# Differential attention with a gated feed-forward: packed diagonal blocks, value projections moved, work redistributed over the units

## The reference, cut to what matters

```python
xn = layernorm(x)                                   # x: 1 x 1024 x 256, float32
q1, k1, q2, k2, v = split(xn @ Wqkv)                # 16 heads; q, k: 8 wide; v: 16 wide
A1 = softmax(causal(q1 k1^T / sqrt(8))) @ v
A2 = softmax(causal(q2 k2^T / sqrt(8))) @ v
diff = A1 - lam * A2                                # lam from four vectors of 8
diff = 0.8 * normalise(diff) ; attn = diff @ Wproj  # rms norm over the 16 values of a head (0.8 stands for 1 - LAMBDA_INIT)
ffn = (gelu(fp8(xn) @ fp8(Wg0)) * (fp8(xn) @ fp8(Wg1))) @ fp8(Wlin)
out = x + attn + ffn
```

## Time and profile before

| | |
|---|---|
| median of 3 runs | 198.92 us (198.6 to 199.15) |
| profiled execution, its own time | 199.27 us |
| its span, first to last instruction | 197.5 us |
| PE busy | 182.2 us, 92% |
| ACT busy | 163.6 us, 83% |
| DVE busy | 92.4 us, 47% |
| POOL busy | 59.4 us, 30% |
| first exponential of a unit starts | 38.01 us |
| last exponential of a unit ends | 180.5 us |
| last value product ends | about 182.75 us |

### The profile page before, as it was taken

One profiled execution on the slowest core, in us unless ns is written; L12 is line 12 of the kernel. 1 busy time (PEld: TensorE's weight loads), 2 busy tenths in 40 slices (PEclk: granted clock), 3 DMA queues, 4 the chain that ended last, 5 costly groups with the idle time before them and its releaser, 6 DMA issues.

```text
span 197.5 us, 3554 instructions
## 1 busy us (share of the span) xinstructions
PE 182.2 (92%) x1446; PEld 78.3 (40%) x1450; DVE 92.4 (47%) x218; ACT 163.6 (83%) x136; POOL 59.4 (30%) x71
## 2 busy tenths in 40 slices
PE   6899989899999999999989999999998999899940
PEld 6855334454332323242333424344342423233830
DVE  0975798431223240540472025216703697895840
ACT  2156865899999999999999999999999899998010
POOL 8526600042216142314442043235216124320000
PEclk9999999999999999999999999999999999999997
DMA  5967377780000000000277781000000000000051
GB/s 174 404 242 245 73 179 205 207 190 10 0 0 3 0 0 3 0 0 3 60 203 188 181 191 39 0 3 0 0 3 0 0 3 0 0 3 0 0 178 44
DMA packets 8149, 14.99 MB, mean 76 GB/s; under 512 B 1984, under 2 KB 5312, under 8 KB 8128
## 3 DMA queue, kind: packets, MB, share of 16 engines
q1 hardware_dynamic: 7440, 14.05, 25.5%
q10 hardware_dynamic: 688, 0.66, 1.0%
HBM read 5.26 MB, written 1.05 MB: 32 GB/s over the span
## 4 chain that ended last, share of the span: by engine, by line
PE 74%; ACT 15%; DVE 4%; POOL 1%; issue 1%; POOLq 0%; DVEq 0%
PE ps L910 29%; PE ps L898 17%; ACT probs L442 13%; PE ps L752 8%; PE ps L758 4%; PE ps L941 4%; PE ps L747 3%; PE ps L851 3%; PE ps L813 3%; DVE area L529 2%; DVE o_t L594 1%; ACT probs L430 1%; PE ps L742 1%; PE ps L947 1%; ACT L430 1%
## 5 line engine op out<-in xcount | busy, mean ns | idle before, releaser
L442 ACT ACTIVATE probs<-ps,shift 128x1536 f32<-128x1536 f32 x96 | 140.1, 1554 | 2.4 <-PE ps L898 1.6
L910 PE MATMUL ps<-probs,v_all 128*32 128x512 f32 (+3 forms) x768 | 78.1, 496 | 1.5 <-DVE o_t L594 1.5
L366 POOL TENSOR_SCALAR_AFFINE_SELECT probs<-probs 128x1024 f32<-128x1024 f32 (+1 forms) x40 | 36.7, 917 | 109.7 <-ACT probs L442 109.6
L898 PE MATMUL ps<-q_st,k_st 32*128 32x512 f32 (+3 forms) x384 | 49.8, 420 | 1.2 <-issue 0.8
L898 PEld LDWEIGHTS ps<-q_st,k_st 32*128 32x128 f32 x384 | 22.4, 182 | 58.6 <-ACT probs L442 30.4
L594 DVE STREAM_TRANSPOSE o_t<-ps 128x512 f32<-128x512 f32 x16 | 11.5, 717 | 49.5 <-PE ps L910 49.5
L910 PEld LDWEIGHTS ps<-probs,v_all 128*32 128x32 f32 x768 | 16.4, 108 | 19.6 <-issue 13.9
L752 PE MATMUL ps<-xn_t,w_q 128*128 128x512 f32 (+1 forms) x38 | 17.3, 557 | 0.8 <-ACT xn_t L393 0.8
L813 PE MATMUL ps<-area 128*128 128x512 fp8e4 x64 | 14.5, 379 | 1.0 <-DVE area L529 1.0
L430 ACT ACTIVATE probs<-ps 128x512 bf16<-128x512 f32 x16 | 9.3, 597 | 4.5 <-PE ps L813 2.7
L529 DVE TENSOR_TENSOR area<-ps,probs 128x512 fp8e4<-128x512 f32 x16 | 10.5, 687 | 1.8 <-ACT probs L430 1.7
(11 more groups left out here) (78 smaller groups left out, 117.2 us busy)
## 6 DMA issues: line engine op xcount, KB each, us to landing
q_st<-parts SPq DMA_DIRECT2D x32, 128.0 KB, 2.8
k_st<-parts SPq DMA_DIRECT2D x32, 128.0 KB, 2.8
probs<-L_ffn_w_gating SPq DMA_DIRECT2D x4, 512.0 KB, 7.8
probs<-L_ffn_w_linear SPq DMA_DIRECT2D x1, 1024.0 KB, 13.1
w_q<-L_attn_Wqkv SPq DMA_DIRECT2D x2, 384.0 KB, 5.8
out<-probs SPq DMA_DIRECT2D x3, 256.0 KB, 3.0
x_sb<-L_attn_x SPq DMA_DIRECT2D x2, 256.0 KB, 4.2
x_sb<-L_attn_x ACTq DMA_DIRECT2D x2, 256.0 KB, 4.5
```

The lines of the kernel that those rows point to most:

```text
L366: pool.affine_select(out=blocks, in_=blocks, pattern=pattern, compare_op=ALU.is_ge, fill=0.0, base=0, channel_multiplier=-1).then_inc(mask ...
L442: act.activation(probs[:, at:at + PER_UNIT, :].rearrange("p s u -> p (s u)"), ps[:, 3 * (n % 2):3 * (n % 2) + 3, :].rearrange("p b n -> p ...
L898: ins = pe.matmul(ps[:, bank, at:at + wide * P], k_st[rows, g % STACKS, kb * P:(kb + 1) * P], q_st[rows, g % STACKS, queries], start=True, ...
L910: ins = pe.matmul(ps[32 * j:32 * j + 32, 6, q0 % HALF:q0 % HALF + wide * P], v_all[:, g % HG, kb, 32 * j:32 * j + 32], probs[:, slot + j, ...
```

## The change

The rows of x are laid on partitions in another order. Of each 256 rows, quarters of 64: even blocks hold quarters 0 and 1, odd blocks quarters 3 and 2. The two halves of a diagonal block that still need masking can then share columns: for two diagonal blocks (256 columns) only 192 are kept, with the first 64 queries of the one in the upper 64 partitions and those of the other in the lower 64. Two groups of heads are laid out together, in 17 chunks of 512 columns where there were 18. Four pairs of groups give 68 chunks, 272 items, and 92 units: 90 of three items, one of one and one of two at the middle.

- A chunk with diagonals has nine pieces: eight of 64 columns and one of 128. So `score` issues nine matmuls per head, two of them with 64 keys as weights and the others with 128. The value product reads the shared strips twice, with two sets of values (`FULL`, and `EARLY`, which has zeros in one half of the partitions).
- There are four such chunks in each pair of groups, and POOL masks each with two instructions on 64 partitions, each over 4 heads, 4 strips and 64 columns.
- Value weights are 17 columns wide, not 32.
- The value projections of blocks 2 to 7 are ahead of the feed-forward part on PE, and ACT copies them out of PSUM, where DVE did. DVE makes the `EARLY` set with four copies.
- The projections of branch 2's queries and keys begin in unit 0, each in one matmul group of 512 columns; norms and down projections have other units, and a down projection is no longer split over two units.
- The loads of x and the stores of the result are twice as many, each of 64 partitions.

```diff
-VW = 32
+VW = DV + 1
+def diagonal(at, a, c):
+    b, d = a + 1, c + 1
+    return [(at, b, FULL, b * P, MINOR), (at + 64, d, FULL, d * P, MINOR),
+            (at + 128, b, EARLY, b * P + MINOR, MINOR), (at + 128, a, EARLY, a * P, MINOR),
+            (at + 192, d, EARLY, d * P + MINOR, MINOR), (at + 192, c, EARLY, c * P, MINOR),
+            (at + 256, a, FULL, a * P + MINOR, MINOR), (at + 320, c, FULL, c * P + MINOR, MINOR)]
 CHUNKS = [
+    [(0, 0, diagonal(0, 0, 2) + [(384, 2, FULL, 384, 128)])],
+    [(0, 0, [(0, 0, FULL, 128, 384), (384, 1, FULL, 256, 128)])],
+    [(0, 0, [(0, 1, FULL, 384, 128)]), (0, 1, [(128, 4, FULL, 640, 384)])],
+    [(0, 1, [(0, 0, FULL, 512, 512)])],
...
+MASKED = (0, 7, 9, 11)
+OPENS = ((0, 0), (2, 1), (8, 1), (10, 1))
+CLOSES = ((2, 0), (8, 0), (10, 0), (16, 0))
+STARTS = list(range(0, ITEMS // 2, 3)) + [ITEMS // 2] + list(range(ITEMS // 2 + 2, ITEMS, 3)) + [ITEMS]
+QK_AT = {0: (4, 0), 1: (4, 1), 5: (5, 0), 8: (5, 1), 13: (6, 0), 17: (6, 1), 25: (7, 0), 29: (7, 1)}
+NORM_AT = {4: 0, 12: 1, 21: 2, 33: 3}
+DOWN_AT = {37: 0, 41: 1, 45: 2, 49: 3, 54: 4, 58: 5, 62: 6, 66: 7}
+LATER = {20: 6, 26: 6, **{k: 4 for k in range(57, 63)}, 63: 3, 64: 3, 65: 3, 66: 2, 67: 2}
+def due(k):
+    return last_unit(k) + LATER.get(k, 5)
...
# SP (the loads by ACT and the stores are doubled in the same way)
+            for i in (0, 2):
+                for p0, rows in halves:
+                    sp.dma_start(x_sb[p0:p0 + MINOR, 2 * i:2 * i + 2, :], x_rows[:, i, rows, :]).then_inc(x_in[i], 16)
# POOL
+                for p0, first in ((0, 0), (MINOR, P)):
+                    strips = probs[p0:p0 + MINOR, at:at + J, first:first + 4 * MINOR].rearrange(
+                        "p j (s u) -> p j s u", s=4)
+                    pool.affine_select(out=strips, in_=strips, pattern=[[0, J], [0, 4], [1, MINOR]],
...
# ACT
+            upper(3)
+            square_of(3)
+            for b in (2, 4, 6):
+                values_in(b)
# DVE
+                for p0 in (0, MINOR):
+                    first = b + p0 // MINOR
+                    dve.tensor_copy(v_all[p0:p0 + MINOR, EARLY, :, first:first + 3:2, :],
+                                    v_all[p0:p0 + MINOR, FULL, :, first:first + 3:2, :]).then_inc(early_out, 1)
# PE, ahead of the feed-forward part
+            for b in range(2, TB):
+                if b >= 4 and b % 2 == 0:
+                    pe.wait_ge(v_out, b - 2)
+                project_values(b)
# PE, scores
+                for p in range(max(len(h) for h in heads)):
+                    for h in heads:
+                        if p < len(h):
+                            ins = score(*h[p], general)
+            def score(g, j, bank, piece, general):
+                at, kb, part, q0, wide = piece
+                rows, queries = slice(32 * j, 32 * j + 32), slice(q0, q0 + wide)
+                keys = MINOR if part == EARLY and kb % 2 == 0 else P
+                out = ps[0:keys, bank, at:at + wide]
+                ins = pe.matmul(out, k_st[rows, g % STACKS, kb * P:kb * P + keys], q_st[rows, g % STACKS, queries],
+                                start=True, stop=not general)
# PE, values
+                for at, kb, of, q0, wide in pieces:
+                    for j in range(J):
+                        ins = pe.matmul(ps[32 * j:32 * j + VW, 6, q0 % HALF:q0 % HALF + wide],
+                                        v_all[:, of, g % HG, kb, VW * j:VW * j + VW], probs[:, slot + j, at:at + wide],
+                                        start=first, stop=False, skip_group_check=True)
+                    first = False
# PE, beside a unit
-                for b in V_AT.get(n, ()):
+                    ins = queries_keys(u, 7, k, 0, HALF)
```

More of the change, by code:

```diff
@@ L686, in _ @@
             bound(dve, own, 1)
+            keep(2, 1)
+            down(0)
             keep(3, 0)
@@ L904, in scores @@
-                ins.then_inc(scores_ready, 1)
-            def product(g, c, at, kb, wide, q0, start):
-                slot = (g * NC + c) % KEPT * J
-                for j in range(J):
-                    ins = pe.matmul(ps[32 * j:32 * j + 32, 6, q0 % HALF:q0 % HALF + wide * P],
-                                    v_all[:, g % HG, kb, 32 * j:32 * j + 32], probs[:, slot + j, at:at + wide * P],
-                                    start=start, stop=False, skip_group_check=True)
-                return ins
@@ L931, in second_half @@
-            def second_half(g):
-                first, (kb, wide, q0) = CHUNKS[MIXED]
-                pe.wait_ge(o_taken, 2 * g + 1)
-                product(g, MIXED, first[1] * P, kb, wide, q0, True)
+                heads = []
+                for e, item in enumerate(range(STARTS[n], STARTS[n + 1])):
+                    k, j = item // J, item % J
+                    heads.append([(2 * (k // NC) + gi, j, 3 * (n % 2) + e, piece)
+                                  for gi, _, pieces in CHUNKS[k % NC] for piece in pieces])
@@ new lines, in values @@
+            def values(k, part):
+                c, slot = k % NC, k % KEPT * J
+                gi, h, pieces = CHUNKS[c][part]
+                g = 2 * (k // NC) + gi
+                if c in MASKED:
+                    pe.wait_ge(masked, masks_until(k))
+                else:
+                    pe.wait_ge(exp_done, last_unit(k) + 1)
+                if k == 0:
+                    pe.wait_ge(v_ones, 1)
+                    pe.wait_ge(zeros_set, 1)
+                    pe.wait_ge(v_out, TB)
+                    pe.wait_ge(early_out, 2)
+                if k == 7:
+                    pe.wait_ge(early_out, 4)
+                first = (c, part) in OPENS
+                if first and (g, h) != (0, 0):
+                    pe.wait_ge(o_taken, 2 * g + h)
+                for at, kb, of, q0, wide in pieces:
[4 more added lines that the diff above has]
+                    first = False
+                if (c, part) in CLOSES:
+                    ins.then_inc(o_ready, 1)
@@ L950, in values_due @@
             def values_due(n, first, end):
-                for g in range(first, end):
-                    for c in range(NC):
-                        if due(g, c) == n:
-                            values(g, c)
-                        if c == MIXED and due(g, c) + 1 == n:
-                            second_half(g)
+                for k in range(first, end):
+                    for part in range(len(CHUNKS[k % NC])):
+                        if due(k) + part == n:
+                            values(k, part)
             def attention(br, general):
```

325 lines of the change are left out of this document (147 added, 178 removed).

## The result

The changed kernel takes **224.59 us** (median of 4 runs, 224.16 to 225.72), beside 199.03 us (198.6 to 199.22) for the kernel before on the same chip: ratio 1.130, 95% interval 1.126 to 1.133. The forecast was 217, its range 203 to 226. The direction and the main cause were right; the size was 7.6 us short. The profiled execution's span went from 197.54 to 223.2 us, +25.7.

What follows compares the result with a forecast made beforehand. The prediction took PE as the bound from unit 6 on, ACT 4% behind; terms 5.3 ahead, 0 in units 0 to 5, 12.4 from unit 6 and 1.0 ending sum to +18.7, 217.6, said as 217 us, range 203 to 226.

Steps and rivals of the forecast that it cites:

- The rival at 192: Whole kernel: ACT sets the pace, so packing its exponentials shortens the units, 192 us; chance 0.09 with mixtures near it.
- Scores: 0.93 us for a unit with a diagonal: PE's scores: weight loads pace nine short pieces, so a diagonal unit takes 0.93 us against 0.43.
- the term +12.6: PE's scores from unit 6 on: longer diagonal units add 12.6 us, of +13.5 over all units.
- the rival at 206 to 207 us: PE's scores: short pieces cost only their columns, so the kernel takes 206 to 207 us; chance 0.15.
- Values: 1.25 for a diagonal chunk: PE's value products: 640 columns and 18 steps make 1.25 us a diagonal chunk, +0.7 us in all.
- The feared floor of 0.107 for a set of four heads: Value products: no set under 0.107 us, +14; with 64-column weights draining PE as alternative, 230 to 236 us, chance 0.11.
- the lower bound I had kept: Value products: 17-column weights could save the first load's 0.03 us, 80 times, -1 us.
- Transposition waits: +3.5: PE at the bank's transposition, from unit 6 on: 7 more waits of 0.5 us, +3.5 us.
- Ahead of the units: +5.3: Before the units: 24 value-projection matmuls +5.2, earlier gelu -0.4, more loads of x +0.5, together +5.3 us.
- Units 0 to 5: 0: First units: ACT sets the pace, so the value projections leaving PE buy nothing, 0 us.
- the clock 0.03: PE's clock falls to 1.2 GHz in stretches of short pieces, over 225 us; chance 0.03.
- Ending: +1.0: End of the kernel: twice as many stores on SP, partly hidden by the additions, +1.0 us.

Runs made afterwards that it cites:

- values_back: Changed kernel with the value projections of blocks 2 to 7 back beside units 0 to 5, copied out by DVE: median 224.66 us.
- long_first: Changed kernel with the 128-column piece of a diagonal chunk first among a head's nine score pieces, not last: 226.57 us.
- before_vw17: Kernel before with value weights of 17 columns, not 32, and nothing else changed: 198.25 us against 199.25.
- opens_later: Changed kernel with products of chunks lying over two accumulation halves further apart, closing part one unit earlier, opening part one later: 224.56 us.
- before_short_pieces: Kernel before with scores of two of a group's nine chunks in eight matmuls of 64 columns per head, not one of 512: 217.37 us.

## Why the prediction was right, and where its size came short

Parts measured by themselves: short score pieces 17.1 us (in the changed kernel), value projections ahead 6.5 and transfers 2.3 (in the kernel before). Together 25.9, of 25.6 measured. That they meet so well is partly luck, because the parts do not simply add: taken out of the changed kernel, the move of the value projections gives nothing by the median (values_back), or 1.7 us once the short pieces are gone. With both undone 6 us remain, of which the transfers are 2.3. The other 4 belong to the rest (values read twice, masks in two instructions, projections in other units), and they were not taken apart.

**PE is the bound, ACT is not.** Shown for the changed kernel. ACT's idle time before the exponentials grew to 22.9 us, and with the score pieces and the start undone the packing bought 0.7 us from unit 6 on. The rival at 192 fell. But with them undone PE is no bound either: both have some 122 us of work in 131.7. The rival went by ACT's sum alone, and what the engines wait for each other was not in it.

**Scores: 0.93 us for a unit with a diagonal.** The mechanism is shown twice, by narrower weights (1.04 to 0.72) and by short pieces in the kernel before (0.43 to 1.01). The value was 1.04, so the term +12.6 was too small by about 30 x 0.11 = 3.3 us, which is what the whole stretch from unit 6 on was short by. (By its own figures the prediction's term is 56.8 - 42.9 = 13.9, and 12.9 from unit 6 on, not 13.5 and 12.6; that hides 0.3 of it.) Three things in the records make the 0.11. A set of three 128-column loads follows the last at 0.112, not 0.107, so the ninth load starts at 0.78, not 0.75. Its matmul starts 0.03 after it, not 0.06. And the last matmul's start is followed by the next work's only 0.24 us later, where I had counted 0.107 for its columns. The mis-sized step is this tail, and it is not the time of the last piece's columns: after a last piece of 64 columns (long_first) it is still 0.21. What it is made of no run here shows.
The Trainium skill (TensorE: Matmul & The Clock Gate, LDWEIGHTS) gives the time of a weight load as its columns over 1.2, in ns, whatever the number of rows: 107 for 128 and 53 for 64 columns. The trace agrees, 0.112 and about 0.058 between sets. The rule cited in the prediction (the Trainium skill, TensorEngine Tiling (Array Packing), Instruction Overhead) is that a matmul of one column takes as long as one of 60; it says nothing of the load. Here the load decides, and the rival at 206 to 207 us fell. The Trainium skill (TensorEngine Tiling (Array Packing), Key Properties) says that a change of tiling mode drains the engine. Between 128- and 64-column loads no drain shows: the ninth load starts at 0.78 us, which is six steps of 0.112 and two of 0.058.

**Values: 1.25 for a diagonal chunk.** Measured 1.24. The feared floor of 0.107 for a set of four heads isn't there: a 64-column set takes half of it. Normal products gained 0.013 by the 17-column weights, worth 1.0 us by themselves (before_vw17), the lower bound I had kept.

**Transposition waits: +3.5.** They came, 3.9 us in 7 places by the view of waits, where it was 1.5 in 3. What the time owes to them is not shown: opens_later left 4.2 us of them in place and was 1.5 us faster up to unit 70.

The stretch's other terms (whole projections -3.7 and -0.4, a norm -0.3) were not measured one by one.

**Ahead of the units: +5.3, measured +6.0.** The 24 matmuls took 5.18, as said. The loads of x were the term mis-sized: four issues on SP take 2.99 us, where two took 0.95, and the first projection starts 1.06 us later, not 0.5.

**Units 0 to 5: 0, measured +2.1.** This is the step that failed in kind. "ACT sets the pace, so they buy nothing" was right of the matmuls, and wrong of what their leaving does. In the changed kernel PE is idle for most of 48 to 50 us, and the clock falls:

```profile
46.00:48.00 2.00, 1.61 (x14) 0.60 (x12) 1.82 (x5) 2.00 (x2) 0.85 (x1) 1.00 0.07 14
48.00:50.00 2.00, 0.50 (x3) 0.19 (x3) 0.10 (x1) 2.00 (x3) 1.85 (x3) 0.82 0.00 0
50.00:54.10 4.10, 2.81 (x7) 0.90 (x8) 0.69 (x1) 3.03 (x3) 0.64 (x1) 0.50 0.00 0
54.10:57.00 2.90, 2.90 (x79) 2.07 (x78) 0.00 (x0) 1.54 (x1) 0.00 (x0) 0.66 0.00 0
```

At 1.2 GHz a projection took 2.08 us instead of 1.06, scores 0.73 instead of 0.43, the first diagonal values 1.81 instead of 1.24. I had given the clock 0.03, and looked for its fall in stretches of short pieces. It fell where PE had too little to do. The same was shown in the kernel before, by moving the six projections away and nothing else. All seven profiles with the value projections ahead have this fall, and none of the six that have them beside the units. Beside it stands a wait of 2.1 us for the squares, which POOL now makes behind a mask twice as long; I had called POOL hidden and had not looked at what else its queue carries in the first units. Taking it away brought unit 6 forward by 1.0 us (2.0 by the medians of the whole), and the clock fell all the same.

**Ending: +1.0, measured +2.1.** The work on PE is the same as before; the stores take longer. But 2.1 is one execution's figure. From the end of the last value product to the end of the span it takes 14.7 to 14.9 us in the four profiles with five stores and 14.8 to 17.0 in the nine with ten, on average 1.0 more. So the term was right on average, and the profile after shows a long one.

## What to carry to other kernels

Where a matmul has fewer columns than the weights in front of it, count loads and their width, not columns: with weights of 128 columns, eight pieces of 64 took 1.01 us where one of 512 took 0.43. Before work is moved off a matmul engine that seems to have it for nothing, ask whether the engine stays busy without it: in the kernel before the move cost 5.2 us where the work went and another 1.3 where it had been. Where two engines are within a few per cent of each other, work taken from the one behind gives next to nothing (7.6 us of ACT's, 0.7 of the stretch), and a sum for each engine alone is too low: with 122 us of work for both the stretch took 131.7.

## What the runs showed of the hardware

- The clock of PE fell to its lower level behind light stretches: from 49 to 56 us in the changed kernel (and from 48 to 55 when the squares came earlier), and from 45 to 55 us in the kernel before without its value projections beside the units. Twice it fell at 180 us (long_first, opens_later), behind ten microseconds in which exponentials set the pace and PE was busy 8.6 and 8.5 of 10.2 us. The changed kernel's profiled execution has the same ten microseconds, with the same 8.6, and its clock stayed up; why it fell in the one and not in the other is open. In the 32 units of short pieces in before_short_pieces, with PE busy 78.78 of 80 us, it never fell.
- The packed kernels vary more: 221.25 to 225.92 us for one of them, roughly in the order of its mean clock, where the kernel before stays within 1.2 us. Falls of the clock in some executions and not in others can make that, and so can the doubled transfers: with them alone the kernel before varies by 2.5 us, and the endings in the profiles by 2.2. The two were not told apart.
- Weight loads of successive pieces of one head, on the same rows of the array, followed each other at 0.112 us while the 64-column matmul between them streamed. One behind the other would have been about 0.112 + 0.053 (an estimate; 0.053 is an eighth of the 0.43 us of 512 columns). So the matmuls lay under the loads.
